# Row maxima of the next half window in two waves around the scores, PSUM banks listed by expected release

## The reference

```python
# layer 0: one head of 32 channels per image
score = jnp.einsum('bcn,bcm->bnm', th, ph)
lat = jnp.einsum('bnm,bcm->bnc', jax.nn.softmax(score, axis=-1), g)
# layer 2: group norm, 8 heads of 32 channels per image
qkv = jnp.einsum('oc,bct->bot', w_qkv, group_norm(x2)) + b_qkv[None, :, None]
weight = jax.nn.softmax(jnp.einsum('bct,bcs->bts', q * scale, k * scale), axis=-1)
a = jnp.einsum('bts,bcs->bct', weight, v)
out = x2 + jnp.einsum('oc,bct->bot', w_proj, a.reshape(B, C, T)) + b_proj
```

## Time and profile before

| what | value |
|---|---|
| median of the runs | 1922.83 us |
| the profiled execution | 1920.26 us |
| its span, first to last instruction | 1918.5 us |
| TensorE busy | 1702.5 us, 89% |
| VectorE busy | 1374.5 us, 72% |
| GpSimd busy | 1357.7 us, 71% |
| ScalarE busy | 787.1 us, 41% |
| granted TensorE clock, mean | 0.940 |

### The profile page before, as it was taken

One profiled execution on the slowest core, in us unless ns is written; L12 is line 12 of the kernel. 1 busy time (PEld: TensorE's weight loads), 2 busy tenths in 40 slices (PEclk: granted clock), 3 DMA queues, 4 the chain that ended last, 5 costly groups with the idle time before them and its releaser, 6 DMA issues.

```text
span 1918.5 us, 37187 instructions
## 1 busy us (share of the span) xinstructions
PE 1702.5 (89%) x15160; PEld 773.6 (40%) x15160; DVE 1374.5 (72%) x2153; ACT 787.1 (41%) x1546; POOL 1357.7 (71%) x581
## 2 busy tenths in 40 slices
PE   5897765799999999999999999999997678889974
PEld 2332222344344444344344344444442345555541
DVE  5677567887777877767867877777771158878875
ACT  0352401155455555455455455455555233333320
POOL 0573600088788887887888878878789059989996
PEclk8898887799999999999999999999998889999986
DMA  5000030220001001001001010010010211222211
GB/s 189 1 2 1 2 129 0 84 77 23 2 2 67 2 2 67 2 9 60 2 24 45 2 59 11 1 67 2 2 45 1 89 29 55 88 77 75 74 51 47
DMA packets 48432, 75.11 MB, mean 39 GB/s; under 512 B 30804, under 2 KB 31110, under 8 KB 48262
## 3 DMA queue, kind: packets, MB, share of 16 engines
q1 hardware_dynamic: 38758, 72.15, 10.6%
q10 hardware_dynamic: 9504, 0.59, 0.3%
HBM read 44.87 MB, written 25.17 MB: 37 GB/s over the span
## 4 chain that ended last, share of the span: by engine, by line
PE 77%; DVE 13%; issue 3%; ACT 2%; DMA 2%; POOL 1%; SPq 1%; POOLq 0%; DVEq 0%; ACTq 0%
PE AV L652 14%; DVE MX L1292 7%; PE S L626 6%; PE RB L895 6%; PE S L688 4%; PE S L603 3%; PE AV L908 3%; PE RB L626 3%; PE RB L944 3%; PE S L638 2%; PE RB L603 2%; PE S L630 2%; PE S L678 2%; PE RB L688 2%; PE S L634 2%
## 5 line engine op out<-in xcount | busy, mean ns | idle before, releaser
L1201 POOL TENSOR_TENSOR ACC<-ACC,PR 128x1024 f32<-128x1024 f32 x360 | 840.9, 2373 | 34.4 <-ACT PR L1034 34.4
L1034 ACT ACTIVATE PR<-S 128x512 f32<-128x512 f32 x667 | 358.6, 603 | 373.1 <-PE S L638 242.9
L1292 DVE TENSOR_REDUCE MX<-S 128x1 f32<-128x512 f32 x646 | 409.4, 681 | 124.2 <-PE RB L603 60.5
L1201 POOL TENSOR_TENSOR ACC<-PR 128x1024 f32<-128x1024 f32 x72 | 168.9, 2368 | 343.0 <-ACT PR L1034 131.6
L652 PE MATMUL AV<-PR,VT 128*32 128x512 f32 x2304 | 312.9, 616 | 3.8 <-ACT PR L1034 3.3
L1292 DVE TENSOR_REDUCE MX<-RB 128x1 f32<-128x512 f32 x336 | 218.5, 681 | 73.8 <-PE S L603 57.0
L1034 ACT ACTIVATE PR<-RB 128x512 f32<-128x512 f32 x328 | 183.7, 604 | 168.9 <-PE S L638 63.4
L626 PE MATMUL S<-HI 32*128 32x512 f32 x667 | 195.6, 493 | 6.2 <-DVE NMR L1305 2.5
L1227 POOL TENSOR_TENSOR PR<-WO,WRK 128x1792 f32<-128x1792 f32 x32 | 155.6, 4883 | 27.9 <-DMA WO<-WO 12.9
L1227 POOL TENSOR_TENSOR PR<-WO,VT 128x1792 f32<-128x1792 f32 x32 | 155.0, 4867 | 10.3 <-DMA WO<-WO 8.3
L603 PE MATMUL S<-HI 32*128 32x512 f32 x646 | 156.2, 507 | 3.4 <-ACT PR L1034 2.8
(11 more groups left out here) (357 smaller groups left out, 3250.9 us busy)
## 6 DMA issues: line engine op xcount, KB each, us to landing
X<-out_y SPq DMA_DIRECT2D x24, 1024.0 KB, 5.0
out_y<-X SPq DMA_DIRECT2D x16, 1024.0 KB, 4.9
X<-in_x SPq DMA_DIRECT2D x8, 1024.0 KB, 8.5
OHU<-out_y SPq DMA_DIRECT2D x8, 512.0 KB, 4.4
X<-out_y SPq DMA_DIRECT2D x8, 512.0 KB, 4.1
out_y<-X SPq DMA_DIRECT2D x8, 512.0 KB, 3.1
out_y<-OHU SPq DMA_DIRECT2D x8, 512.0 KB, 3.1
WO<-WO SPq DMA_DIRECT2D x128, 16.0 KB, 1.9
```

The lines of the kernel that those rows point to most:

```text
L1034: nc.scalar.activation(exps(s, pair)[:, HALF * one:HALF * one + HALF], RING[ring.place()], ACT.Exp, scale=1.0 if i is None else float(D) * ...
L1201: nc.gpsimd.tensor_tensor(ACC[:, pair, :], so_far, exps(s, pair), ALU.add).then_inc(pool_used, 1)
L1292: nc.vector.tensor_reduce(out=MX[:, h, t, keys:keys + 1], in_=bank(), op=ALU.max, axis=AX.X).then_inc(ring_free, 1)
```

## The change

1. `maxima` now lists sixteen "max" jobs for a half, each two heads of one tile of 128 queries by 512 keys: first all tiles against the first 512 keys, then against the second. `window_jobs` puts one of them into each of the first seven steps as "max", and one or two (`LATE`) as "late"; these come after all other jobs of the step.
2. On TensorE the "max" wave of a step stands directly behind the scores, before the values; the other jobs stand behind the values, the late waves last. VectorE works in the order max, other jobs, late.
3. The ring no longer goes round. `Ring.begin` names the banks of a step ahead: from a list of free banks, and when it is empty from the banks of this same step, in the order in which they are expected to come free; what is left over is the list for the next step.
4. The V product is two jobs of four tiles instead of four of two, so VectorE adds the bias to 512 columns at a time. The QK jobs move to steps 0, 2, 8 and 10 (in the first layer they stay), the post jobs to steps 3, 5, 12 and 15, gn jobs by one step.
5. The semaphore `stage_ready` goes; TensorE waits on the count of the QK bank's own release (`kept_qk`).

```diff
     def __init__(self):
-        self.at, self.slots = 0, tuple(range(SLOTS))
+        self.free, self.step = list(range(SLOTS)), []
 
     def place(self):
-        self.at += 1
-        return self.slots[(self.at - 1) % len(self.slots)]
+        if self.step:
+            return self.step.pop(0)
+        self.free.append(self.free.pop(0))
+        return self.free[-1]
...
+    def begin(self, jobs, single):
+        held = []
+
+        def take():
+            if not self.free:
+                self.free.append(held.pop(0))
+            self.step.append(self.free.pop(0))
+            return self.step[-1]
+
+        for _ in range(H):
+            held.append(take())
+        for job in jobs:
+            for n in range(places(job, single)):
+                slot = take()
+                held.insert(2 * n + 1 if job[0] == "max" else len(held), slot)
+        self.free += held
...
-    return {"max": 4, "stats": 0, "negate": 0, "reread": 0, "concepts": 4, "softmax": 0, "turn": 4,
+    return {"max": 2, "late": 2, "stats": 0, "negate": 0, "reread": 0, "concepts": 4, "softmax": 0, "turn": 4,
...
-QK_ORDER = ((1, 0), (1, 1), (0, 0), (0, 1))
+QK_ORDER = ((1, 0), (0, 0), (1, 1), (0, 1))
+LATE = (1, 2, 1, 1, 2, 1, 1)
...
-    return [("max", half, t, keys) for t in range(TILES_HALF) for keys in range(2)]
+    return [("max", half, n) for n in range(4 * TILES_HALF)]
...
-            for n, tile in enumerate(maxima(1 - half)):
-                jobs[first + (n if n <= SUM_AT else n - 1)].append(tile)
+            waves = maxima(1 - half)
+            for n, count in enumerate(LATE):
+                jobs[first + n].append(waves.pop(0))
+                late[first + n] = [("late",) + waves.pop(0)[1:] for _ in range(count)]
             jobs[first + MT - 1] += [("negate", 1 - half), ("flip", 1 - half)]
         if half == 1 or trail:
-            jobs[first + SUM_AT].insert(1, ("sums",))
+            jobs[first + SUM_AT].append(("sums",))
             jobs[first + SPREAD_AT].append(("spread", half - 1))
     if nxt:
-        for step, job in zip((1, 2, 3, MT + (3 if post or gn or single else 7)), QK_ORDER):
+        for step, job in zip((1, 2, 3, MT + 3) if single else (0, 2, MT, MT + 2), QK_ORDER):
             jobs[step].append(("qk",) + job)
-        parts = (6, MT + 1) if single else (7, MT + 1, MT + 1, MT + 2) if gn else (4, 6, 7, MT + 2)
-        for n, step in enumerate(parts):
+        for n, step in enumerate((6, MT + 1) if single else (4, 7) if gn else (3, 7)):
             jobs[step].append(("v", n))
     if post:
-        for step, job in zip((4, 6, MT + 4, MT + 7), ((0, 0), (1, 0), (0, 1), (1, 1))):
+        for step, job in zip((3, 5, MT + 4, MT + 7), ((0, 0), (1, 0), (0, 1), (1, 1))):
             jobs[step].append(("post",) + job)
     if ahead:
         first = MT + 3 if ahead == 2 else MT
         jobs[first].append(("stats", 0, ahead))
         jobs[first + 1].append(("stats", 1, ahead))
-        jobs[first + 2].append(("gn", 0, ahead))
+        jobs[first + (2 if ahead == 2 else 3)].append(("gn", 0, ahead))
     if gn:
-        jobs[MT + 4].append(("gn", 1, 1))
-    return jobs
+        jobs[MT + 5 if ahead else MT + 3].append(("gn", 1, 1))
+    for step, stage in side:
+        jobs[step].append(stage)
+    return [job + waves for job, waves in zip(jobs, late)]
...
+            def max_scores(u, par, half, n):
+
+                keys, t, pair = n // (2 * TILES_HALF), n // 2 % TILES_HALF, n % 2
+                if n % (2 * TILES_HALF) == 0:
+
+                    wait(pe, ring_free, max(kept_qk[u, 0, half], kept_qk[u, 1, keys]))
                 first = HALF * half + P * t
-                for h in range(H):
+                for h in (2 * pair, 2 * pair + 1):
                     mm(bank(), HI[par][D * h:D * h + D, 0, first:first + P],
...
             def window(u, par, jobs, i):
                 for s in range(STEPS):
+                    ring.begin(jobs[s], i is None)
                     scores(u, par, s)
-                    if s:
-                        values(u, par, s - 1)
-                    elif ("sums",) in jobs[SUM_AT]:
-                        values(u - 1, 1 - par, STEPS - 1)
-                    for job in jobs[s]:
-                        if job[0] == "spread":
+                    behind = [job for job in jobs[s] if job[0] != "max"]
+                    for job in jobs[s][:len(jobs[s]) - len(behind)] + [("values",)] + behind:
+                        if job[0] == "values" and s:
+                            values(u, par, s - 1)
...
-                if which == 0:
-                    own()
-                    dve.sem_inc(stage_ready, 1)
...
-            def keep_v(u, par, part, bias, n=2):
-                src = bank()
+            def keep_v(u, par, part, bias):
+                src, n = bank(), 4
...
-            def row_max(half, t, keys):
-                for h in range(H):
+            def row_max(half, n):
+                keys, t, pair = n // (2 * TILES_HALF), n // 2 % TILES_HALF, n % 2
+                for h in (2 * pair, 2 * pair + 1):
```

More of the change, by code:

```diff
@@ L70, in __init__, with reset @@
     def __init__(self):
-        self.at, self.slots = 0, tuple(range(SLOTS))
+        self.free, self.step = list(range(SLOTS)), []
     def place(self):
-        self.at += 1
-        return self.slots[(self.at - 1) % len(self.slots)]
+        if self.step:
+            return self.step.pop(0)
+        self.free.append(self.free.pop(0))
+        return self.free[-1]
     def skip(self, n):
[L78 to L82, removed]
+        for _ in range(n):
+            self.place()
+    def reset(self):
+        self.free = list(range(SLOTS))
     def only(self, slot):
-        self.at, self.slots = 0, (slot,)
+        self.free = [slot]
+    def begin(self, jobs, single):
[12 more added lines that the diff above has]
+        self.free += held
 def places(job, single):
@@ L99, in wait, with window_jobs @@
         eng.wait_ge(sem, value)
-QK_ORDER = ((1, 0), (1, 1), (0, 0), (0, 1))
+QK_ORDER = ((1, 0), (0, 0), (1, 1), (0, 1))
+LATE = (1, 2, 1, 1, 2, 1, 1)
 def maxima(half):
-    return [("max", half, t, keys) for t in range(TILES_HALF) for keys in range(2)]
-def window_jobs(post=False, nxt=True, gn=False, ahead=0, trail=True, single=False):
+    return [("max", half, n) for n in range(4 * TILES_HALF)]
+def window_jobs(post=False, nxt=True, gn=False, ahead=0, trail=True, single=False, side=()):
     jobs = [[] for _ in range(STEPS)]
+    late = [[] for _ in range(STEPS)]
     for half in range(2):
@@ L154 @@
 AFTER_AT = (3, 3, 4, 5, 5, 6, 7, 7, 8, 9, 10, 10, 11, 12, 13, 13, 14, 15)
-START = [("v", 0)] + maxima(0)[:4] + [("v", 1)] + maxima(0)[4:] + [("negate", 0), ("flip", 0), ("weights",)]
+START = [("v", 0)] + maxima(0)[:8] + [("v", 1)] + maxima(0)[8:] + [("negate", 0), ("flip", 0), ("weights",)]
 def after_jobs():
-    jobs = window_jobs(nxt=False)
+    jobs = window_jobs(nxt=False, side=[(3, ("spread", -1))] + list(zip(AFTER_AT, AFTER)))
     jobs[SPREAD_AT].remove(("spread", -1))
-    jobs[3].append(("spread", -1))
-    for step, stage in zip(AFTER_AT, AFTER):
-        jobs[step].append(stage)
     return jobs
@@ L177, in first_jobs @@
             ("classes",): [("qk",) + job for job in QK_ORDER[2:]],
-            ("norms",): [("v", n) for n in range(4)]}
-    for stage, n in ((("pool",), 3), (("hidden",), 2), (("gates",), 2), (("regate",), 1)):
+            ("norms",): [("v", n) for n in range(2)]}
+    for stage, n in ((("pool",), 6), (("hidden",), 4), (("gates",), 4), (("regate",), 2)):
         jobs[stage] = tiles[:n]
@@ L578, in all_read, with placed_l0 @@
                 wait(pe, ring_free, drained.now())
-            def qk_l0(g, which, half):
+            def placed_l0(g, which, half):
                 dst = bank()
@@ L587, in qk_l0 @@
                 last.then_inc(ring_full, 1)
+            def qk_l0(g, which, half):
+                placed_l0(g, which, half)
+                kept_qk[g, which, half] = drained.now()
             def v_l0(g, part):
-                qk_l0(g, 2, part)
+                placed_l0(g, 2, part)
                 all_read()
@@ L645, in values @@
                     wait(pe, half_kept, 2 * (2 * u + half) - 1)
-                if half == 0 and (u < 2 and mt == 0 or u > 1 and mt % 2 == 0):
-                    wait(pe, v_ready, 2 * (u + 1) if u < 2 else 4 * u - 3 + mt // 2)
+                if half == 0 and (u < 2 and mt == 0 or u > 1 and mt % 4 == 0):
+                    wait(pe, v_ready, 2 * (u + 1) if u < 2 else 2 * u + 1 + mt // 4)
                 wait(pe, exp_done, EXPS * u + H * s + H)
@@ L674, in v_product @@
                     pe.wait_ge(wv_in, 16)
-                for m in range(2):
-                    mt = 2 * part + m
+                for m in range(4):
+                    mt = 4 * part + m
                     for t in range(CT):
@@ L680, in v_product, with qk_product @@
                 last.then_inc(ring_full, 1)
```

(5 more changed lines are left out.)

38 lines of the change are left out of this document (19 added, 19 removed).

## The result

The changed kernel takes 2010.19 us (median of four runs, 2009.76 to 2015.07) against 1923.64: a ratio of 1.0463, with a 95% interval from 1.0434 to 1.0491. It is 87 us slower. Forecast were 1991 us and 1942 to 2038. The profiled execution took 2010.5 us, with a span of 2008.7, against 1920.26 and 1918.5.

What follows compares the result with a forecast made beforehand. TensorE bounds the kernel, busy 1702.5 of 1918.5 us; after the change its early wave waits for VectorE. Seven iterations at +9.9 us (+69) and +2 outside, on 1920.3, gave 1991 us, range 1942 to 2038.

Steps and rivals of the forecast that it cites:

- the one on banks: With seven banks, the early wave gets the job's bank and first late bank, so QK steps take 5.67 us.
- The step without a job: Step with two late maxima and no job: scores' third bank frees 1.53 us after values start; period 2.65 against 3.40.
- The sum: All step periods of one iteration added: 149.7 us against 139.8, +9.9 times 7, plus 2 outside.
- the clock: TensorE's granted clock falls after pauses, about 1.6 us each; thirty falls cost 48 us: 2040 us, chance 0.07.
- the even window's second post step (step 5): Residual step: next early wave waits for VectorE's eviction and first late maximum; period 4.80 us.
- the odd window's group sums: Step where VectorE's statistics stand before the late maxima, so the early wave waits behind them: 3.21 us.
- the main case: The prediction's own forecast, slower through the early wave's wait for VectorE: 1991 us, chance 0.68.
- the last window: Outside the seven iterations, the last window loses job-free waits: -3 us.
- The first even window: Outside the seven iterations, this window has QK steps but no residuals: +2 us.
- the first layer's first window: Outside the seven iterations, this window has three QK steps that grow: +3 us.
- The rule against the rows: Each TensorE mode change costs about 0.10 us; one fewer in some 20 steps would gain 2.0 us per iteration.
- No VectorE chain: Late maxima's banks free in time, only TensorE's work left: 123.5 us per iteration, 1806 us; faster, chance 0.11.

Runs made afterwards that it cites:

- The banks' order: The changed kernel with the early banks entered behind the four scores' banks in the list of releases instead of between them: 2022.12 us in one run.

## Why the prediction was right

**Sign and mechanism.** The step that carried it was the one on banks: seven banks, four for the scores, so that the early wave can only have the job's bank and the first late one. The timeline shows just that: in the QK step the second head starts 2.29 us after the late wave, forecast 2.3. Four experiments hold it from four sides: the late waves moved (-103 us), the early wave moved (QK step 4.70), the split made longer (+0.60 for 0.60), the waves undone (-9.9 us of 13.8 an iteration).

**The terms.** Values to values, forecast and measured: QK 5.67 and 5.63; sums 5.76 and 5.61; post 4.80 and 4.84; V 4.88 and 5.10; V with four late 6.09 and 6.29; post with four late 6.02 and 6.03; spread 3.36 and 3.41; without a job 2.65 and 2.71, with four late 3.91 and 3.89; flip and V 4.51 and 4.60; flip and post 4.36 and 4.54; flip alone 3.43 and 3.68; statistics 3.97, 5.39 and 3.95, 5.66; group sums of the even window 2.84 and 3.02. The step without a job came close by luck, as said under "The banks' order". Of the 0.15 by which the sums are shorter, 0.12 stand between values and sums: 0.88 us from the one's start to the other's, 1.00 from values to anything else. Both work in column tiles; that no change of mode is needed is my reading of it. The V steps are 0.2 longer because VectorE waits after the addition for its own write before it reports V: the next maximum starts 0.14 after its end, where others start 0.08 before the end of the one ahead. That wait was in the code (`own()` in `keep_v`) and I had not priced it.

**The size: +71 forecast, +90 measured.** The forecast started from the profiled execution of the kernel before, 1920.3 us; the profiled one after took 2010.5 (the medians are 87 apart). The sum had seven iterations of +9.9 us and +2 outside. Cut the same way, the seven measured +96.6, 13.8 each, and the rest -6.4.

The term of the iteration that was mis-sized is the clock, which the sum had at nothing. Two steps miss by more than 0.3 us: the even window's second post step (step 5), forecast at 4.80 and measured at 6.47, and the odd window's group sums, 3.21 and 4.32. Both hold a fall of the clock. That is 2.8 of the 3.9 us by which an iteration (149.7 forecast, 153.6 measured) was short. In the run with the double late wave moved, the same two steps without a fall take 4.84 and 3.43 us, so 2.5 of the 2.8 are the clock's. I had the clock as a rival of its own, with thirty falls and 2040 us; it came as a part of the main case, with twelve in six iterations.

Outside the seven iterations the last window lost 2.9 us of waits, as forecast (3). The first even window was forecast at +2 and measured -0.3, the first layer's first window at +3 and -0.8. There the QK steps did grow by the chain, from 4.43 to 5.46 us, but the steps without a job and with two late maxima fell from 3.40 to 2.70 and the first step by 1.4, which the sum had left out. That the outside was 8 us too high took back a part of the 27 us by which the iterations were too low: 1991 stands closer to the measured time by luck.

**The rule against the rows.** A wave of maxima takes 0.43 us ahead of a product of another kind and 0.34 ahead of the scores, and the sums saved 0.12; both fit a price of about 0.1 us for a change of TensorE's mode, which no run here tests by itself. That it must wait for a drain is what the Trainium skill says (TensorEngine Tiling (Array Packing), Key Properties), without a price. The switches that the change saves were no gain in its total, since the early wave waited for VectorE instead.

**Rivals.** "No VectorE chain" did not happen to the change but is nearly what the late waves ahead of the job make of its QK steps. Those versions take 1907 and 1880 us, not the 1806 of that rival: each job step still pays the late wave's 0.43 in front of the job (QK 4.70 us, not 4.50), and the steps with statistics, the flip steps and the job-free step with four late maxima (3.89 us) still wait.

## What to carry to other kernels

When work is split into an early and a late part, ask of each bank of the early part whose read frees it, and count the queue of that reader: here a wave of two matmuls made its step 1.15 us longer (5.63 against the 4.48 without it) because the late part had been put behind the job and VectorE reads in order. Put what the other engine must read ahead of the long product, not behind it, so that the reading runs beside it. Compare the rounds of a loop by the time from one fixed instruction to the next; the busy shares of this kernel moved by 2 to 4 points and named no cause.

## What the runs showed of the hardware

The granted clock of TensorE (1.00 is 2.4 GHz, 0.51 is its level of 1.2 GHz) fell after short waits in an engine that was busy nearly throughout: 5.84 of 6.30 us busy by the profile, and then 3.4 us at 0.51, in the same step of each iteration. The longest idle time of TensorE in those 6.30 us stands between the scores' third and fourth head, which start 0.84 us apart:

```profile
847.14 0.49 PE L655 MATMUL S<-HI 32*128 32x512 f32 x1
847.98 0.49 PE L655 MATMUL S<-HI 32*128 32x512 f32 x1 [0.34 <-DVE MX L1324]
```

Moving the double late wave by one step took the clock from twelve falls to four.

The Trainium skill has a case like it (TensorE: Matmul & The Clock Gate, A second HAM failure mode: psum-queue depth-cycling): a kernel that works through its PSUM banks in turn, with frequent very short idle stretches of TensorE between groups of matmuls, sees its clock swing between half and full. The trace agrees in kind, with the numbers above. What makes one pattern of waits bring a fall and the next not is open: the runs show where, not why.
